# Product 1 ahead of product 0 in the expert slots of a four-layer kernel

## The reference, cut to what matters

```python
weights = _router_weights(x, Wr, temperature)          # x: 4 x 256 tokens of 512 -> here 4 x 512 tokens
gate = einsum('btd,edf->ebtf', x, Wg)                  # 8 experts, 512 -> 512
up   = einsum('btd,edf->ebtf', x, Wu)
gate[:2] += einsum('btd,edr,erf->ebtf', x, Ga, Gb)     # low-rank part of experts 0 and 1
up[:2]   += einsum('btd,edr,erf->ebtf', x, Ua, Ub)
mid = silu(gate) * up
out = einsum('ebtf,efd->ebtd', mid, Wd)                # [:2] has a low-rank part too
x = layernorm(x + einsum('bte,ebtd->btd', weights, out))
```

## Time and profile before

| | |
|---|---|
| median of 3 runs | 2333.25 us (2330.73 to 2336.75) |
| the profiled execution, its own time | 2334.09 us |
| its span from first to last instruction | 2332.4 us |
| mean granted clock of TensorE, share of full speed | 0.99 |
| slot 1 starts at | 1318.4 us |
| a plain slot (one of 18 to 31) | 29.92 us |

### The profile page before, as it was taken

The page is one execution under the profiler, slowest core; times in us unless marked ns, Lnnn a source line. Parts: engine busy times, 40 slices in busy tenths (PEclk is TensorE's granted clock), DMA queues, the critical chain, the costliest instruction groups (busy, mean ns, idle before and its releaser), DMA issues.

```text
span 2332.4 us, 30825 instructions
## 1 busy us (share of the span) xinstructions
PE 2268.7 (97%) x10746; PEld 1862.8 (80%) x10746; DVE 1573.5 (67%) x2385; ACT 880.1 (38%) x1436; POOL 761.1 (33%) x570
## 2 busy tenths in 40 slices
PE   8999999999999999999999899999999999999997
PEld 7887888888868888888877787778778778888885
DVE  5567777777778765683446666667677886666765
ACT  5456333333343222321222543324344444444441
POOL 0003544444413222341212532324234543333331
PEclk9999999999999999999999999999999999999999
DMA  6856222222250100000000211221011111111110
GB/s 214 227 157 176 64 73 72 75 73 72 59 204 1 37 19 19 23 1 19 1 1 28 82 55 55 81 90 74 28 55 55 55 67 51 54 54 54 54 36 36
DMA packets 92199, 154.36 MB, mean 66 GB/s; under 512 B 6320, under 2 KB 56496, under 8 KB 85824
## 3 DMA queue, kind: packets, MB, share of 16 engines
q1 hardware_dynamic: 92096, 153.02, 20.0%
HBM read 113.68 MB, written 39.32 MB: 66 GB/s over the span
## 4 chain that ended last, share of the span: by engine, by line
PE 62%; DVE 5%; issue 2%; ACT 1%; POOL 1%; POOLq 0%; DVEq 0%; ACTq 0%
PE attn_pvk L1235 4%; PE attn_pvk L1236 4%; PE attn_pvk L1237 4%; PE attn_pq L1235 2%; PE attn_pq L1236 2%; PE attn_pq L1237 2%; PE attn_po L1235 2%; PE attn_pv L1235 2%; PE attn_po L1236 2%; PE attn_po L1237 2%; PE attn_pv L1236 2%; PE attn_pv L1237 2%; PE attn_pv L85 2%; PE attn_pv L87 2%; PE attn_pv L86 2%
## 5 line engine op out<-in xcount | busy, mean ns | idle before, releaser
L2657 DVE TENSOR_TENSOR moe_a_lo<-moe_up_raw,moe_a_hi 128x512 fp32r<-128x512 f32 x192 | 183.1, 969 | 154.7 <-ACT moe_a_hi L2120 154.7
L2002 POOL TENSOR_TENSOR moe_h_lo<-moe_c_t,moe_h_hi 128x512 fp32r<-128x512 f32 x96 | 128.3, 1336 | 354.7 <-ACT moe_h_hi L2120 354.6
L1235 PE MATMUL attn_pvk<-moe_b_hi,moe_a_hi 128*128 128x512 f32 x512 | 201.7, 394 | 13.9 <-ACT moe_c_last L2246 6.0
L1237 PE MATMUL attn_pvk<-moe_b_hi,moe_a_lo 128*128 128x512 f32 x512 | 200.5, 392 | 0.0
L1236 PE MATMUL attn_pvk<-moe_b_lo,moe_a_hi 128*128 128x512 f32 x512 | 200.4, 391 | 0.0
L2120 ACT ACTIVATE moe_c_t<-attn_pvk 128x512 f32<-128x512 f32 x192 | 113.2, 596 | 186.7 <-PE attn_pvk L1237 184.7
L1349 POOL TENSOR_TENSOR ffn_h_lo<-ffn_h_f,ffn_h_hi 128x512 fp32r<-128x512 f32 x64 | 92.8, 1452 | 241.5 <-ACT ffn_h_hi L1416 241.5
L1593 DVE SCALAR_TENSOR_TENSOR all_acc<-attn_pvk,ffn_wts,all_acc 128x512 f32<-128x512 f32 x128 | 91.2, 749 | 93.2 <-PE attn_pvk L87 88.3
L2172 ACT ACTIVATE moe_c_t<-moe_c_t 128x512 f32<-128x512 f32 x96 | 60.4, 630 | 240.7 <-DVE moe_c_t L2729 240.7
L2120 ACT ACTIVATE moe_a_hi<-moe_up_raw 128x512 fp32r<-128x512 f32 x192 | 116.0, 625 | 56.4 <-POOL moe_up_raw L1972 56.4
L1235 PEld LDWEIGHTS attn_pvk<-moe_b_hi,moe_a_hi 128*128 128x128 f32 x512 | 96.7, 189 | 38.1 <-issue 11.3
(11 more groups left out here) (504 smaller groups left out, 6548.3 us busy)
## 6 DMA issues: line engine op xcount, KB each, us to landing
moe_up_raw<-in_e_up SPq DMA_DIRECT2D x28, 1024.0 KB, 5.7
moe_dn_raw<-in_e_dn SPq DMA_DIRECT2D x28, 512.0 KB, 3.7
xh<-mix_out_hi SPq DMA_DIRECT2D x32, 256.0 KB, 2.6
zs<-mix_out_z SPq DMA_DIRECT2D x32, 256.0 KB, 3.5
xl<-mix_out_lo SPq DMA_DIRECT2D x32, 256.0 KB, 3.9
mix_x<-xh SPq DMA_DIRECT2D x16, 512.0 KB, 4.1
mix_x<-xl SPq DMA_DIRECT2D x16, 512.0 KB, 5.3
mix_z_raw<-zs SPq DMA_DIRECT2D x16, 512.0 KB, 3.9
```

The lines of the kernel that those rows point to most:

```text
L1235: pe.matmul(out, lh, rh, start=first, stop=False, skip_group_check=True)
L1237: return pe.matmul(out, ll, rh, start=False, stop=True, skip_group_check=True)
L2002: tt(h_lo[:, m, tok], src, raw(h_hi[:, m, tok]), ALU.subtract).then_inc(s_hlo, 1)
L2657: tt_(a_lo[q][:], src, raw(a_hi[q][:]), ALU.subtract).then_inc(s_alo, 1)
```

## The change

In every slot but slot 0, `up` of product 1 is issued ahead of `up` of product 0; the `down` products keep their places. So the order on TensorE becomes q1, d0, q0, d1, q2, and so on (in slot 1: q1, q0, q2). Every wait on the count of finished products (`s_up`) is told the new place of its product by `place_of`; the other engines keep their own orders.

```diff
+        TURN = (1, 0, 2, 3, 4, 5, 6)
...
+        place_of = lambda n, q: q if at(n, 0) else TURN[q]
...
-                reach(act, s_up, 14 * (n - 1) + 2 * q + 2)
+                reach(act, s_up, 14 * (n - 1) + 2 * place_of(n - 1, q) + 2)
                 copy(a_hi[q][:], src).then_inc(s_ahi, 1)
...
-                    act.wait_ge(s_up, 14 * (SLOTS - 1) + 2 * q + 2)
+                    act.wait_ge(s_up, 14 * (SLOTS - 1) + 2 * place_of(SLOTS - 1, q) + 2)
...
             def take(n, i, q, sem, tile, low):
 
-                act.wait_ge(s_up, 14 * n + 2 * q + i + 1)
+                act.wait_ge(s_up, 14 * n + 2 * place_of(n, q) + i + 1)
...
-                for q in range(7):
+                for step in range(7):
+                    q = step if at(n, 0) else TURN[step]
                     for i in range(2):
                         if not (at(n, 0) and (q, i) in FIRST):
                             up(n, q, i)
-                    for c in downs(n)[q]:
+                    for c in downs(n)[step]:
...
-                dve.wait_ge(s_up, 5 if at(n, 0) and (q, i) == (1, 1) else 14 * n + 2 * q + i + 1)
+                dve.wait_ge(s_up, 5 if at(n, 0) and (q, i) == (1, 1) else 14 * n + 2 * place_of(n, q) + i + 1)
```

## The result

The changed kernel takes 2383.44 us (median of 4 runs, 2382.45 to 2386.02) against 2333.81 for the kernel before beside it: 1.0212 of it, 95% interval 1.0200 to 1.0225, so 49.6 us slower. The forecast was 2375, 41.7 slower. The profiled execution took 2382.96 us with a span of 2381.2, 48.8 over the span of before.

A forecast was written before the change was run, and what follows sets the result against it. TensorE, busy 97% of the span, was taken as the bound, slowed where VectorE returns banks late. Waits of 29.8 us plus 11.9 for the clock made 41.7, on 2333.25: 2375 us, range 2352 to 2397.

The forecast's parts named there:

- Plain slots: In 21 slots the ring's bank returns late for d2: 0.15 us wait plus 0.11 refill, 0.26 each, 5.5 us.
- Slot 1: At slot 1, which has no early down, the wait for X goes: 1.0 us gained.
- Slots 5 to 8: TensorE waits at merge 1 for the bank and d1 starts late: 4.6, 4.5, 3.4 and 4.5 us, together 17.0.
- Slots 10 and 11: The second transpose and the second logits wait for the late bank: 3.2 us and 4.1 us.
- Slots 13 and 15 to 18: Slot 13's gain is given back at d2; slots 15 to 18 lose little: together 1.0 us, bounds -2 and 5.
- I expect it 1.4 earlier: In slot 16, the VectorE sum that d2 waits for ends 1.4 us earlier, against 1.9 of new lateness from slot 15.
- The clock: After TensorE waits of about 4 us in slots 5 to 8, 10, 11, 13, half clock costs 1.7 each, 11.9 us.
- faster: VectorE's chain does not decide, banks return in time, only lost waits for X remain: 2318 us, chance 0.05.
- the 15 us that the order was to win: Product 0's waits for the old contents of X, with refills and a slow clock behind one, put at 15 us.
- The clock holds: TensorE's new waits come but its clock stays at full speed: 2363 us, chance 0.17.
- `down_low` stays at 2.31: GpSimd's work shifts along and still shuts VectorE out in 21 plain slots, 1.1 us more each: 2398 us, chance 0.09.
- the signs given: In the profile: moe_c_last waits gone, new 4 us waits in slots 5 to 8, plain slots 30.2 us, more clock dips.

The follow-up runs named there:

- the filled waits: Changed kernel plus 15 matmuls nobody needs between product 0 and the second merge in slots 5 to 8: 2376.66 us, 1.0180 of the kernel before.
- the casts first in the new order: Changed kernel with ScalarE's up_high of product 6 and down_high ahead of product 0's takes, slot 16's late splits moved behind: 2328.64 us, 0.9975 of before.
- the ranking moved as well: New order, those two casts ahead of the takes, the ranking's last two parts moved from slot 12's end into slot 13: 2321.90 us, again 2322.12.
- the old order gave back 1.6: Changed kernel with the old order of products in slots 13, 15, 16 and 17: 2375.43 us, 1.0181 of the kernel before.

## Why the prediction was right

The direction, the place and the mechanism were right; the size was 8 us short, within the range. The term that was mis-sized most is the clock: 11.9 us forecast, 15.9 measured.

1. *Plain slots.* Forecast 0.26 us each in 21 slots, 5.5 in all; measured 0.30 in 21 slots, 6.2 in all. They are not quite the same 21: slot 15 had the loss too, and slot 13, which was counted, had none, for its d2 waits for the ranking (33.01 us after product 3 of slot 12, before 33.00). The 1.22 for `down_low` held (1.23), and the bound of 2.31 with it did not come. The refill (a first matmul of 0.50 us behind a wait) costs 0.14, a little more than the 0.11 that the longer duration showed. That this is the bank is shown by `down_low` behind the turn.
2. *Slot 1.* Forecast -1.0, measured -1.01.
3. *Slots 5 to 8.* Forecast 17.0 for the bank. By d1's start, counted from product 3 of the slot before, it was 4.7, 4.5, 4.6 and 4.5: 18.3. Slot 7 was mis-sized: its old wait for X of 1.0 was not won, for d0 now waited 1.0 for the `add_down` of slot 6's last `down`. Both waits have one cause, which the order of products does not touch: in slot 6 GpSimd's sum waits for the store of the merged weights, and then runs beside two splits of VectorE, which take 2.38 us and not 1.28 as in slot 7, so that all behind them on VectorE is 1.1 late:

```profile
1518.17 1.82 POOL L1970 TENSOR_TENSOR moe_up_raw<-moe_up_raw 128x512 f32<-128x512 f32 x1 [5.59 <-DMA e_dn_m<-moe_dn_raw]
1518.15 2.38 DVE L2660 TENSOR_TENSOR moe_a_lo<-moe_up_raw,moe_a_hi 128x512 fp32r<-128x512 f32 x2
```

GpSimd waited 5.78 us there before, 3.84 with the filled waits, where d0 did not wait. With the casts first in the new order slot 7 took 36.94 us when that wait was 3.81, and with the ranking moved as well 38.01 when it was 5.66. Why the store takes longer in slot 6 of some executions stays open.

4. *Slots 10 and 11.* 3.2 and 4.1 forecast; 3.2 and 4.1 measured, without the clock.
5. *Slots 13 and 15 to 18.* In slot 13 the gain was given back as forecast; d2 waited for the bank there:

```profile
1774.04 0.50 PE L1235 MATMUL attn_pq<-moe_dn_hi,moe_h_hi 128*128 128x512 f32 x1 [4.29 <-DVE all_acc L2692]
```

For slots 15 to 18 the forecast was 1.0, and 2.7 came (4.7 from 15-16 to 17-18, less 0.3 for a plain slot and 1.7 for the clock). The step that failed is "I expect it 1.4 earlier" of slot 16. The two casts of slot 16 did come 1.1 earlier from the slot's start, and `down_low` with them, but then `down_low` took 2.28 us beside a GpSimd sum, and not 1.21 as before:

```profile
1873.00 2.28 DVE L2670 TENSOR_TENSOR moe_dn_lo<-moe_dn_raw,moe_dn_hi 128x1024 fp32r<-128x1024 f32 x1
1875.20 0.74 DVE L2692 SCALAR_TENSOR_TENSOR all_acc<-attn_pq,moe_wts,all_acc 128x512 f32<-128x512 f32 x1
```

The bank came back 18.3 us after the slot's start, as before from the time when slot 15 had run out (the earlier trace rows less 1815.0). Slot 15 itself ran out 2.4 later than before, where 1.9 was forecast. Here the bound that did not come in plain slots did come.

6. *The clock.* Forecast seven falls at 1.7 us, 11.9. It fell in all seven, and behind slot 16's d2 too, where the wait was 4.0 us: 15.9 in all, 2.2 to 2.7 in each of slots 5 to 8 (9.8), 1.1 in slot 10, 1.7 in 11, 1.6 in 13, 1.7 in 16. The term was mis-sized in slots 5 to 8, since the slow stretch in slot 5 was 6.9 us and not 3.5, and it left out slot 16. (Before, the clock fell in slot 16 as well, to 0.50 from 1821.5 to 1825.5 behind the waits for X of 2.6 and 2.0 us, but there d2 had to wait for its bank anyway, so nothing was lost by it.) That the 9.8 are the clock is shown by the filled waits, which gave 8.3 back and kept a fall of 1.5 in slot 8. In slot 13 the old order gave back 1.6. For slots 10, 11 and 16 it is read from the length of the steps alone. One reading was off: TensorE stood for 3.2 us at the end of slot 0's product 3, and not 3.4, which counts one regular step of 0.23 in. And the length of a wait did not decide as the forecast supposed: the clock fell behind waits of 2.5 us and held behind one of 3.2.

Sum: 6.2 - 1.0 + 18.3 + 3.2 + 4.1 + 2.7 + 15.9 = 49.4, the table's 49.36; before slot 0's product 3 the changed kernel was 0.5 faster, which makes the 48.8 of the spans.

The rivals: *faster* needed a bank that comes back in time, which the kernels with the casts first have. Of the 15 us that the order was to win, it won nothing in them (2328.64 against 2327.16) and 6.8 with the ranking moved, since at first waits of 8.5 us for `add_down` took the place of those for X. *The clock holds* and *`down_low` stays at 2.31* fell, the second in all slots but 16: `down_low` took 2.24 to 2.31 us in 24 of the 32 slots before, and 1.22 or 1.23 in 31 of them after.

Of the signs given, one was misread: the waits for `moe_c_last` did not all go; 1.0 us stayed in slot 16, for VectorE's last product. Left open is how long the slow clock lasts after a given wait: after the same 4.0 us in slot 10 it cost 1.1 us in the changed kernel and about 2.4 with the filled waits ahead of it.

## What to carry to other kernels

When a product moves back in TensorE's order, look at what stands behind its reader in the other engines' queues: here two casts that had nothing to do with it, and through them a bank, cost 50 us. With the reader behind them the loss turned into a small gain, though no larger than the same edit gave in the old order; only with the ranking moved as well was the new order worth 6.8 us. Compute when the bank comes back and when it is wanted, for each kind of slot: in a plain slot a shift of 4.1 met 2.7 us of slack and cost only 0.3, because `down_low` no longer ran beside a GpSimd sum and became 1.1 shorter; the slots with one more user of the ring had no slack. A wait that is removed at the head of a slot is a gain only if the next wait isn't for the same late engine.

## What the runs showed of the hardware

In the changed kernel a wait of 4 us on TensorE was followed by the half clock in all eight places, and cost 1.1 to 2.7 us on top; in slot 10 the price differed by 1.3 us from kernel to kernel with the same wait. With `down_low` behind the first turn the clock also fell behind waits of 2.5 us (slots 5 to 8, 10 and 11) but not behind one of 3.2 us (slot 13). 15 unneeded matmuls in a wait of 4 us were cheaper than standing still. A wait of 0.16 us is not on the page, as the modelled end of the last matmul covers it, and costs 0.30: only the distance between slots shows it. The same `down_low` took 1.22 us alone and 2.28 beside a GpSimd sum, and a shift of a few us removed the meeting in 24 slots and made a new one in slot 16.
